# The linear attention stage of a two-layer block: weighing x before v's projection

## The reference, cut to what matters

```python
QKV = einsum('bsd,ed->bse', X, W_in) + b_in       # X is the normalised x
Q, K, V = split(QKV, 3)
Q, K = rope(Q, 128), rope(K, 128)
A = sum(feature_map(K) * V, axis=-2)              # feature_map: K / max(norm(K), 1e-12), per token
Y = einsum('bsd,ed->bse', A[:, None, :] * Q, W_out) + b_out + X
```

## Time and profile before

| | |
|---|---|
| three runs | 585.16, 590.18, 589.98 us (median 589.98) |
| the profiled execution | 586.74 us, span of its instructions 584.9 us |
| granted clock of TensorE, mean | 0.995 |
| last attention batch begins (PE) | 399.64 us |
| rounds 1 to 7 of the linear layer (PE) | 449.80 to 506.2 us |
| first product of the gated layer | 508.17 us |

### The profile page before, as it was taken

One profiled execution on the slowest core, in us unless ns is written; L12 is line 12 of the kernel. 1 busy time (PEld: TensorE's weight loads), 2 busy tenths in 40 slices (PEclk: granted clock), 3 DMA queues, 4 the chain that ended last, 5 costly groups with the idle time before them and its releaser, 6 DMA issues.

```text
span 584.9 us, 12971 instructions
## 1 busy us (share of the span) xinstructions
PE 568.5 (97%) x4180; PEld 535.2 (91%) x4180; DVE 475.9 (81%) x1464; ACT 371.7 (64%) x1041; POOL 222.2 (38%) x326
## 2 busy tenths in 40 slices
PE   8999999999999999999999999999999999899995
PEld 7899999999999999999999999999998888788884
DVE  4689779778967997797789778977887989779875
ACT  5786657656765755576557657567887756554452
POOL 4565223223223432332233233323447878503320
PEclk9999999999999999999999999999999999999998
DMA  8803300000000000000000000000000000001011
GB/s 321 291 1 110 117 2 2 1 1 0 0 0 0 0 0 0 0 0 0 0 0 0 0 0 0 0 0 1 1 1 1 1 2 1 2 1 36 18 37 57
DMA packets 9136, 14.71 MB, mean 25 GB/s; under 512 B 1552, under 2 KB 6672, under 8 KB 9104
## 3 DMA queue, kind: packets, MB, share of 16 engines
q1 hardware_dynamic: 9104, 14.30, 6.9%
HBM read 12.20 MB, written 2.10 MB: 24 GB/s over the span
## 4 chain that ended last, share of the span: by engine, by line
PE 84%; DVE 6%; POOL 3%; ACT 2%; issue 2%; DMA 1%; SPq 0%; POOLq 0%; DVEq 0%
PE bank L624 68%; PE bank L710 5%; PE bank L724 5%; PE bank L727 2%; PE bank L634 2%; DMA raw<-in_wv 1%; PE bank L819 1%; ACT prob L1092 1%; DVE pT L1693 1%; DVE raw L1677 1%; DVE prob L1686 1%; POOL qkv L460 1%; PE bank L888 0%; POOL big L520 0%; POOL x L447 0%
## 5 line engine op out<-in xcount | busy, mean ns | idle before, releaser
L504 POOL TENSOR_SCALAR prob<-prob,rowinv 128x128 f32<-128x128 f32 (+1 forms) x128 | 97.0, 771 | 276.0 <-DVE rowinv L1482 276.0
L624 PE MATMUL bank<-xT,big 128*128 128x256 f32 x984 | 129.3, 283 | 0.3 <-DVE kT L1421 0.3
L624 PEld LDWEIGHTS bank<-xT,big 128*128 128x128 f32 x984 | 123.4, 192 | 1.2 <-DVE kT L1421 0.5
L1092 ACT ACTIVATE prob<-prob,negmax 128x128 f32<-128x128 f32 (+1 forms) x256 | 112.8, 444 | 8.8 <-DVE negmax L1466 8.8
L624 PE MATMUL bank<-wp,oT 128*128 128x256 f32 x768 | 102.3, 283 | 0.0
L624 PEld LDWEIGHTS bank<-wp,oT 128*128 128x128 f32 x768 | 96.9, 190 | 0.7
L1055 ACT ACTIVATE qT<-bank 128x512 fp32r<-128x512 f32 x68 | 40.7, 598 | 75.6 <-PE bank L624 75.5
L624 PE MATMUL bank<-pT,v 128*128 128x512 f32 (+1 forms) x384 | 79.9, 343 | 0.9 <-DVE pT L1421 0.8
L624 PEld LDWEIGHTS bank<-pT,v 128*128 128x128 f32 x384 | 63.1, 189 | 10.5 <-DVE oT L1421 1.0
L1421 DVE TENSOR_TENSOR pT<-bank,pT 128x512 fp32r<-128x512 f32 (+1 forms) x128 | 65.1, 550 | 2.4 <-ACT pT L1055 2.3
L1055 ACT ACTIVATE pT<-bank 128x512 fp32r<-128x512 f32 (+1 forms) x128 | 55.2, 483 | 12.0 <-PE bank L724 9.8
(11 more groups left out here) (163 smaller groups left out, 973.3 us busy)
## 6 DMA issues: line engine op xcount, KB each, us to landing
x<-in_x SPq DMA_DIRECT2D x8, 256.0 KB, 8.0
raw<-in_wq SPq DMA_DIRECT2D x4, 512.0 KB, 8.1
raw<-in_wp SPq DMA_DIRECT2D x4, 512.0 KB, 8.0
out<-x SPq DMA_DIRECT2D x7, 256.0 KB, 2.1
raw<-in_w_gu SPq DMA_DIRECT2D x2, 640.0 KB, 4.8
raw<-in_w_in SPq DMA_DIRECT2D x1, 768.0 KB, 4.5
raw<-in_w_down SPq DMA_DIRECT2D x1, 640.0 KB, 5.7
raw<-in_wk SPq DMA_DIRECT2D x1, 512.0 KB, 3.6
```

The source lines that it names most:

```text
L504: m = pool.tensor_scalar(prob[:, j % 2, 0, a:b], prob[:, j % 2, 0, a:b], rowinv[:, j % 2, r:r + 1], None, ALU.mult)
L624: m = pe.matmul(out, lhs(a), rhs(b), start=first and i == 0, stop=last and i == len(passes) - 1, skip_group_check=True)
L1092: m = act.activation(prob[:, j % 2, i, a:b], prob[:, j % 2, i, a:b], ACT.Exp, scale=-1.0, bias=negmax[:, 2 * i + r:2 * i + r + 1], accum_o ...
```

## The change

k and v part. PE multiplies x with the columns of k only (`linear_k`: both tiles, 256 wide, share one bank), with no bias matmul. DVE copies both tiles of k out of the bank and adds the bias (`k_copy`). ACT squares k from the copy (`k_squares`) and writes `xw`: the normalised x of each token times its inverse norm (`weigh`), with the inverse norm itself as column 257. PE then makes, in plain float32 and not in three passes, the product over the tokens of k with `xw`: 128 features of k by 257, two banks, two tiles each (`linear_sum`). It no longer needs v: v's weights and bias, transposed once by PE and kept in `wv_bias`, are multiplied with that product by DVE, which adds up each row to A (`linear_sum` on DVE, one instruction with a kept sum for each half). v is never made, and neither is DVE's product of k and v nor ACT's copy of A. The output product has three passes in both.

Around it: the normalised x has two buffers; in a round `linear_apply`, `add_bank` and the copy of k now come first; in the last attention batch PE makes the output projection of step 6 ahead of `attend` of step 7, and four transposes of v's weights are new.

The core of the diff (left out: names of semaphores, buffers, the weights' places):

```diff
@@ PE @@
+            def linear_wv():
+                pe.wait_ge(s_vlo, 2 * NB)
...
+                for k in range(KT):
+                    pe.transpose(bM[:, k * P:(k + 1) * P], wv_pairs[:, k, :], ident[:])
+                    m = pe.transpose(bM[:, D + k * P:D + (k + 1) * P], raw_v[:, k, P:D], ident[:])
...
+            def linear_k(n, t):
+                if t == 0:
+                    pe.wait_ge(s_llo, n + 1)
...
+                        pe.wait_ge(s_lke, n - 1)
                 for k in range(KT):
-                    mm3(pe, out[:, :], lambda a: xTs[n % 2][:, a, k, t * P:(t + 1) * P], lambda a: lin_w[:, a, k, D:3 * D],
-                        k == 0, False)
-                pe.matmul(out[:, :], mean_rows, kv_bias, start=False, stop=True, skip_group_check=True).then_inc(s_kvp, 1)
+                    m = mm3(pe, bK[n % 2][:, t * D:(t + 1) * D], lambda a: xTs[n % 2][:, a, k, t * P:(t + 1) * P],
+                            lambda a: lin_w[:, a, k, D:2 * D], t == 0 and k == 0, t == ST - 1 and k == KT - 1)
...
             def linear_sum(n):
-                pe.wait_ge(s_lkv, n + 1)
+                pe.wait_ge(s_lxs, n + 1)
+                pe.wait_ge(s_lr, n + 1)
...
-                        m = pe.matmul(bO[:, e:e + 1], kv[:, t, e * P:(e + 1) * P], ones[:, 0:1], start=t == 0, stop=t == ST - 1)
+                        m = pe.matmul(bA[e][:, 0:D + 1], k_sb[n % 2][:, t, e * P:(e + 1) * P], xw[:, t, :],
+                                      start=t == 0, stop=t == ST - 1)
@@ ACT @@
-            def linear_k(n, t):
...
-                act.activation(k_sb[n % 2][:, t, :], out[:, 0:D], ACT.Copy).then_inc(s_lke, 1)
...
+            def k_squares(n):
+                act.wait_ge(s_lke, n + 1)
+                if n > 0:
                     act.wait_ge(s_lkb, n)
+                for t in range(ST):
+                    m = act.activation(k_square[:, t, :], k_sb[n % 2][:, t, :], ACT.Square, accum_out=k_norm[:, t:t + 1])
...
+            def weigh(n):
+                act.wait_ge(s_lki, n + 1)
+                for t in range(ST):
+                    m = act.activation(xw[:, t, 0:D], xns[n % 2][:, t, :], ACT.Copy, scale=k_inv[:, t])
...
             def linear(n):
-                linear_k(n, 0)
+                if n > 1:
+                    k_squares(n)
+                linear_y(n - 1)
                 linear_x_hi(n + 1, (n + 1) % 2) if n + 1 < NB else gated_x_hi(0)
-                linear_y(n - 1)
-                linear_k(n, 1)
+                weigh(n)
+                linear_q(n)
@@ DVE @@
+            def k_copy(n):
+                dve.wait_ge(s_lkp, n + 1)
...
+                dve.tensor_tensor(k_sb[n % 2], bK[n % 2][:, :].rearrange("p (t d) -> p t d", t=ST),
+                                  b_k.rearrange("p (o d) -> p o d", o=1).to_broadcast([P, ST, D]), ALU.add).then_inc(s_lke, 1)
...
-            def linear_kv(n):
...
-                    m = dve.scalar_tensor_tensor(kv[:, t, :], k_sb[n % 2][:, t, :], k_inv[:, t:t + 1],
-                                                 bKV[n % 2][t][:, D:2 * D], ALU.mult, ALU.mult)
...
+            def linear_sum(n):
...
+                    dve.wait_ge(s_lG, 2 * n + e + 1)
+                    dve.tensor_tensor_reduce(weighted_sums[e], bT[e][:, 0:D + 1], wv_bias[:, e, :], 1.0, 0.0, ALU.mult, ALU.add,
+                                             A_sb[:, e:e + 1]).then_inc(s_lA, 1)
@@ POOL @@
             def k_inverse(n):
...
                 if n > 0:
-                    pool.wait_ge(s_lkv, n)
+                    pool.wait_ge(s_lG, 2 * n)
             def linear(n):
+                if n > 0:
+                    linear_bias(n - 1)
+                k_sine(n)
+                if n == NB - 1:
+                    inv_std(NB + 1)
+                k_inverse(n)
+                k_rotate(n)
...
-                if n < NB - 1:
-                    linear_bias(n + 1)
```

More of the change, by code:

```diff
@@ L451, in ternary_bias, with k_sine @@
                 add_row(n, 0).then_inc(s_fb, 1)
+            def k_sine(n):
+                q = n % 2
+                k = k_sb[q][:, :, 0:P].rearrange("p t (e i) -> p t e i", e=2)
+                sin = rope[:, 1, :, 0, :].rearrange("p t (i e) -> p t e i", e=2)
+                pool.wait_ge(s_lke, n + 1)
+                for e in range(2):
+                    m = pool.tensor_tensor(k_sin[q][:, :, e, :], k[:, :, 1 - e, :], sin[:, :, e, :], ALU.mult)
+                m.then_inc(s_lks, 1)
             def k_rotate(n):
@@ L456, in k_rotate @@
                 k = k_sb[q][:, :, 0:P].rearrange("p t (e i) -> p t e i", e=2)
[L457 to L461, removed]
                 pool.wait_ge(s_lks, n + 1)
                 pool.wait_ge(s_lkc, n + 1)
+                pool.wait_ge(s_lsq, n + 1)
                 pool.tensor_tensor(k, k_cos[q], k_sin[q], ALU.add).then_inc(s_lr, 1)
@@ L784, in batch @@
                         q_project(*ahead(n, j, 3))
+                    if j == 1 and last:
+                        linear_wv()
                     if j == 2 and not (isinstance(n, int) and n == 0):
                         pe.wait_ge(s_vlo, 2 * n + 2)
+                        if last:
+                            pe.wait_ge(s_wv, 1)
                         ternary_transpose(n - 1)
@@ L794, in batch @@
                     if j >= 6 and last:
-                        linear_kv(0, j - 6)
+                        linear_k(0, j - 6)
                     if j == 6 and last:
                         linear_transpose(1)
+                    if j == J - 1 and last:
+                        out_project(n, j - 1)
                     attend(n, j)
-                    if j > 0:
+                    if j > 0 and not (j == J - 1 and last):
                         weights(n, late={1: 3, 3: 5, 5: 7, 7: 8}.get(j, 0))
@@ L1236, in linear_residual, with order_wv, linear_wv, k_bias @@
                 m.then_inc(s_lres1, 1)
-            def kv_bias_hi():
-                act.wait_ge(s_sp, 2 * J * NB)
-                act.activation(mean_rows, ones[:, :], ACT.Copy, scale=1.0 / H)
-                for some, hi in zip(by_pairs(b_in[:, D:3 * D]), by_halves(kv_bias)):
-                    m = act.activation(hi, some, ACT.Copy)
-                m.then_inc(s_bhi, 1)
+            def order_wv():
+                act.wait_ge(s_rawl[0], 16)
+                act.activation(wv_pairs.rearrange("p k (e i) -> p k e i", e=2),
+                               raw_v[:, :, 0:P].rearrange("p k (i e) -> p k e i", e=2), ACT.Copy).then_inc(s_wvo, 1)
+            def linear_wv():
+                act.wait_ge(s_wvp, 1)
+                act.activation(wv_bias[:, :, 0:D], bM[:, :].rearrange("p (e c) -> p e c", e=2), ACT.Copy).then_inc(s_wv, 1)
+            def k_bias():
+                for some, out in zip(by_pairs(b_in[:, D:2 * D]), by_halves(b_k)):
+                    m = act.activation(out, some, ACT.Copy)
+                m.then_inc(s_bk, 1)
             def constants_by_feature():
```

240 lines of the change are left out of this document (122 added, 118 removed).

## The result

The changed kernel is **slower by 1.5%**: 597.42 us median against 589.01, ratio 1.0148 [1.0111, 1.0185]. Its profiled execution took 597.54 us (span 595.7, clock 0.997) against 586.74 (span 584.9): +10.8 us, 1.8%. The two differ by the base: 589.01 is the median of four runs from 585.16 to 590.18 us, and nineteen later runs of the kernel before had a median of 586.8. The forecast was +5.4 and 593.8; the result lies inside the range of 586.5 to 600, and 0.9 above the forecast's own 591 to 596.5. GpSimd is POOL in the rows, ScalarE ACT, VectorE DVE.

The account below looks back on a forecast made before the run. VectorE was taken to bound the linear-stage rounds. The terms -0.6 + 4.5 + 2.4 - 0.9 = +5.4 us, put on 588.4, gave 593.8 us; own range 591 to 596.5, stated range with rivals 586.5 to 600.

Parts of the forecast that it names:

- the ring: Linear-stage rounds: VectorE waits on ScalarE's squares, y, weighing and q's copy before products of q; 7.55 against 6.15 us, +1.40.
- Rounds, +4.5: Five linear-stage rounds: +7.0 us, less 1.1 for a normalisation moved out and 1.4 for slack; ends +0.8 and +5.9.
- ready at 2.1, so hidden: In each round: GpSimd's inverse norm, needed for weighing x, is ready 2.1 us after VectorE's copy of k, hidden by ScalarE's steps.
- Last attention batch, -0.6: Last attention batch: TensorE has 1.8 us less work, partly lost to waits and VectorE's copies of k; -0.6, ends 0 and -1.8.
- Last round, +2.4: From the last copy of k to the gate's first matmul: 9.1 us against 6.70, so +2.4 (1.4 to 3.4).
- Ones-product off the gate, -0.9: Gated layer: the last batch's ones-product no longer stands between the first two gate products, -0.9 us.
- Plain products: TensorE's rounds: four plain float32 matmuls of 257 columns, eight records at 0.22 us, take 1.76 us and stay hidden.
- The rival with twice the price: Rounds: plain products at 0.44 us a record make TensorE's round 8.3 us, past 7.55; 598.5 us, chance 0.11.
- TensorE is no bound here: Answers the rival that TensorE bounds rounds and attention: its round falls from 7.7 to 6.6 us; -8.5, 580 us, chance 0.11.
- Only VectorE's work counts: Rival: ScalarE's steps overlap better, so rounds +0.8, attention -1.8, last round +1.4; about -0.5, 588 us, chance 0.12.
- VectorE and GpSimd collide more: Rival: VectorE's longer round meets GpSimd once more in most rounds; +3.5 us on top, 597 us, chance 0.08.

Follow-up runs that it names:

- the first four experiments: On the changed kernel: plain products issued twice 1.0183; q's copy before weighing 1.0078; GpSimd's bias addition behind k's rotation 1.0059; both moves 0.9995 (ratios to kernel before).
- both edits: Changed kernel with ScalarE's q copy before its weighing and GpSimd's bias addition behind k's rotation: ratio 0.9995 to the kernel before, span 585.2 us.

## Why the prediction was right, and where it was short

The direction held and the ring is there. The size was short: +5.4 us of 10.8 on the profiled execution, of 8.4 by the medians. What was missing is collisions (instructions of VectorE and GpSimd that take longer side by side) and a late inverse norm, together at least as large as the ring (6.8 us came back with the addition moved, 5.5 with q's copy). Two choices helped the number: the forecast stood on 588.4 and not on the profiled 586.74, from which it would have been 592.1 against 597.54; and the stated range held because it took in the rivals' times, while the forecast's own ended at 596.5. By its steps:

- **Ring through ScalarE** (+1.40 a round, VectorE waits ahead of the products of q): held. VectorE waited there in five rounds, 0.47 to 0.82 us in four of them (forecast 0.75), and 0.31 ahead of y's second half; without other work a round took 7.69 (forecast 7.55). The fifth wait, 2.15, has the next step's cause. Taking q out of the ring gave back 5.5 us with what came along.
- **Rounds, +4.5:** measured 48.00 - 41.40 = +6.6, above my end of +5.9. The step that failed is in the ring's list: "ready at 2.1, so hidden". There I counted sine products, bound and power, but not what GpSimd may still have ahead of them. In round n=5 that was a stretched rotation of q, the last batch's mean and scale and the addition of the bias, 1.3 us: the inverse norm was ready at 4.1, and the wait was 2.15 where I had 0.75 (+1.4). The other term that I had too small is what runs beside GpSimd. From start to start four normalisation pairs took 1.60, 1.35, 1.07 and 1.67 against my 1.08 (+1.4). With the addition moved, the first two took 0.66 and 0.65 and the other two stayed, and the cosine products of round n=6 fell by 0.70. These terms make more than the 2.1 us that were missing; the other four waits were shorter than I had them, and the split of the last ternary batch took 1.26 us and no longer 1.78.
- **Last attention batch, -0.6:** wrong in sign. The first marker came at 461.11 against 460.07, +1.0 (in the first four experiments the copy of k before it, at 447.55, came 0.3 to 0.6 earlier, so part of this may be run to run). TensorE did gain, but VectorE's pairs at 449.27 and 458.91 took 1.82 and 1.67 us, by their starts 1.2 more than two of 1.08; with the addition moved and nothing else, the marker stands at 458.96, -1.1, inside my range of 0 to -1.8.
- **Last round, +2.4:** measured 10.32 against 6.70, +3.6, above my end. From start to start the two normalisations took 2.73 us for 1.8, the copy 0.15, the sums (with a wait of 0.31 for y behind them) 0.24 and the splits 0.18 more than my list; statistics and flag took 0.30 less. With the addition moved it took 9.68.
- **Ones-product off the gate, -0.9:** from the first gate matmul to the first output matmul it took 523.21 - 519.43 = 3.78 us, before 4.71 by the same starts: -0.93.
- **Sum:** 1.0 + 6.6 + 3.6 - 0.9 = 10.3. The other 0.5 us of the 10.8 come in the gated layer, and no step of mine has them. The first gate matmul started at 519.43, 11.3 us later than before, where I had 514.5.
- **Plain products:** 0.22 us a record forecast, (1.90 - 0.38) / 7 = 0.217 measured. The rival with twice the price is refuted, and doubling them showed that it would have changed little. The Trainium skill ("FP8 and Floating Point Precision", TensorE Precision Notes) counts four passes for true FP32. Two records of 0.217 make 0.43 a product of 257 columns, near the 0.48 estimated from that count.
- **The rivals:** TensorE is no bound here (products doubled: +1.2 us). "Only VectorE's work counts" fell with the wait of 4.4 us. "VectorE and GpSimd collide more", which I gave 0.08 and +3.5 us, came true on top of the ring, with other instructions than y's pair. It was one mechanism more, not another case, and should have been a term of the sum: the description of the change has the normalisation at the head of VectorE's round, and its diff the addition at the head of GpSimd's.

What stays open: why the gated layer takes 0.5 us more, and whether weighing first can win anything; with both edits its last round still takes 3.0 us more than before.

## What to carry to other kernels

Where one engine's work goes into a ring that passes through a second one, put what the first waits for ahead of whatever waits for a third: that reordering gave 5.5 of 10.8 us back with no work removed. When a new wait hangs on a third engine, list all that its queue holds ahead of it in each round, also what the change leaves in place; and when work moves on VectorE, ask what GpSimd runs beside it, with the length of both. Test a relief on the old kernel as well before the new one gets the credit.

## What the runs showed of the hardware

- An addition of GpSimd over 128x512 (1.3 us) stretches VectorE's pairs that read and write outside the banks: normalisation 0.73 alone, 1.43 to 1.82 beside it; y's low part 0.88 alone, up to 1.98 beside it. So does other work of GpSimd (normalisation 1.75 beside q's rotation and the down weights), and GpSimd's own instructions are stretched as well: q's rotation 0.73 alone, 1.50 beside VectorE's low parts of the down weights. Instructions of VectorE that read a bank keep their time: the addition to x took 0.66 to 0.69 us everywhere, and the copy of k at 501.20 took 0.68 with GpSimd's addition starting at 501.43. The Trainium skill ("GPSIMD Engine Reference", section Specifications) names contention with VectorE instructions of two kinds, in a two-port mode or with two inputs from SBUF. The trace agrees for the second kind (y's low part) and adds the price, up to 1.1 us for 1.3 us of GpSimd's instruction. The normalisation has one input from SBUF; no row shows in which mode it ran.
- VectorE's sum over 257 columns of a bank times a row took 0.41 to 0.42 us and 0.08 for the read of the result, but only 0.34 to 0.35 from start to start: priced at 0.42 each.
- A wait added to one engine made the kernel faster (0.9988 [0.997, 1.0007] to 0.9943 [0.9919, 0.9967]), since it moved 1.3 us a round of GpSimd's work beside VectorE's reads of banks.
